# High halves of five experts' weights fetched by casting DMAs instead of cast on ScalarE

## The reference, cut to what matters

```
h = layernorm(layernorm(patches) @ W_proj + b_proj)          # 576 x 192
h = h + attention(norm(h))                                     # 12 heads, cos() queries, 9 tokens an image
h = h + experts(norm(h)):                                      # 8 experts, top 2 of each token
      logits = x @ router.T;  top_w = softmax(top 2 logits)
      for e in range(8):
          out += (silu(x @ Wg[e].T) * (x @ Wu[e].T)) @ Wd[e].T * w_e
```

## Time and profile before

| | |
|---|---|
| median of 3 runs | 222.52 us (221.71 to 222.67) |
| the profiled execution's own time | 222.33 us |
| its span | 220.4 us, mean granted clock 0.961 |
| PE busy | 190.8 us (87%) |
| DVE busy | 150.8 us (68%) |
| ACT busy | 134.2 us (61%) |
| POOL busy | 131.4 us (60%) |
| DMA | 36.34 MB, mean 165 GB/s |

### The profile page before, as it was taken

The page is one execution under the profiler, slowest core; times in us unless marked ns, Lnnn a source line. Parts: engine busy times, 40 slices in busy tenths (PEclk is TensorE's granted clock), DMA queues, the critical chain, the costliest instruction groups (busy, mean ns, idle before and its releaser), DMA issues. The chain is left out here.

```text
span 220.4 us, 4927 instructions
## 1 busy us (share of the span) xinstructions
PE 190.8 (87%) x1575; PEld 144.4 (66%) x1589; DVE 150.8 (68%) x486; ACT 134.2 (61%) x315; POOL 131.4 (60%) x184
## 2 busy tenths in 40 slices
PE   8999969999697798699578989996999999999940
PEld 2899959999596664464154667673777666667620
DVE  1799798997983899887558977775755555555420
ACT  2654587599969698666868667564544444444430
POOL 8342399999699434869988976784222222222222
PEclk9999999999999999985969999999999999999985
DMA  5999999949852512573787777753511112222111
GB/s 154 372 398 382 355 408 408 386 162 308 240 146 49 150 52 66 149 212 100 203 281 213 239 175 189 191 123 58 118 19 18 20 19 45 42 42 45 18 21 18
DMA packets 22577, 36.34 MB, mean 165 GB/s; under 512 B 4057, under 2 KB 11545, under 8 KB 22553
## 3 DMA queue, kind: packets, MB, share of 16 engines
q1 hardware_dynamic: 19609, 33.26, 47.2%
q0 software_dynamic: 2944, 2.76, 8.6%
HBM read 31.65 MB, written 4.36 MB: 163 GB/s over the span
## 5 line engine op out<-in xcount | busy, mean ns | idle before, releaser
L1383 PE MATMUL ps<-experts 128*117 128x193 f32 (+1 forms) x320 | 54.4, 328 | 0.5 <-ACT experts L816 0.3
L1383 PEld LDWEIGHTS ps<-experts 128*117 128x117 f32 (+1 forms) x320 | 52.1, 180 | 2.0 <-DMA experts<-x_t 1.5
L430 POOL TENSOR_TENSOR experts<-stage,experts 128x528 bf16<-128x528 f32 x36 | 43.2, 1216 | 13.5 <-ACT experts L741 12.8
L1318 DVE TENSOR_TENSOR shared<-shared,ps 128x256 f32<-128x256 f32 x48 | 20.2, 421 | 36.9 <-ACT shared L925 35.3
L741 ACT CAST experts<-stage 128x528 f16<-128x528 f32 x64 | 38.8, 633 | 5.2 <-DMA stage<-w_exp 5.2
L925 ACT ACTIVATE shared<-ps 128x256 f32<-128x256 f32 x48 | 18.5, 385 | 28.4 <-PE ps L1588 26.9
L725 ACT ACTIVATE experts<-experts 128x468 f32<-128x468 f32 x39 | 21.9, 586 | 15.4 <-POOL experts L561 4.0
L685 POOL DMA_INDIRECT out<-shared x8 | 12.4, 1545 | 30.3 <-ACT shared L950 22.8
L561 POOL TENSOR_TENSOR experts<-experts 128x468 f32<-128x468 f32 x14 | 16.5, 1176 | 15.6 <-ACT experts L725 15.4
L685 POOL DMA_INDIRECT out<-shared,slot_row x8 | 14.2, 1775 | 19.4 <-ACT shared L950 16.3
L1609 PE MATMUL ps<-experts,shared 128*128 128x192 f16 (+1 forms) x96 | 23.7, 246 | 1.6 <-DVE shared L1323 1.6
(11 more groups left out here) (241 smaller groups left out, 369.7 us busy)
## 6 DMA issues: line engine op xcount, KB each, us to landing
stage<-w_exp SPq DMA_DIRECT2D x64, 264.0 KB
experts<-x_t SPq DMA_DIRECT2D x12, 472.0 KB, 8.0
experts<-x_t SPq DMA_DIRECT2D x16, 236.0 KB, 6.8
experts<-w_proj SPq DMA_DIRECT2D x8, 384.0 KB, 6.7
slot_x<-experts SPq DMA_DIRECT2D x1, 1032.0 KB, 8.0
shared<-slot_x SPq DMA_DIRECT2D x8, 129.0 KB, 3.3
out<-h SPq DMA_DIRECT2D x1, 351.0 KB
slot_x<-xs,posi POOLq DMA_INDIRECT x10
```

The source lines that it names most:

```text
L430: ops.tensor_tensor(lo_w[:, to + EW:to + EW + PW], stage[:, n % STAGES, :], hi_w[:, to:to + PW], ALU.subtract).then_inc(split_pool if on_p ...
L1318: v.tensor_tensor(hid[:, n % 2, :], act[:, n % 2, :], pcol(n % 3, BLK, BLK), ALU.mult).then_inc(hid_ready, 1)
L1383: last = mm(dst, xbuf[:, t % 2, k, 0:m], gw[:, k, :], start=k == 0, stop=k == KT - 1)
```

## The change

Only ScalarE's high halves of experts 0 to 2 (24 pieces) stay. For experts 3 to 7 GpSimd issues one DMA each, from the float32 weights in HBM to the float16 half in `experts`, which converts on the way. The float32 pieces of these experts are still loaded to `stage`, since the low halves need them. Their split waits for `high_in` of the expert and for its own `stage_in` in place of `hi_done`. GpSimd splits 40 pieces in place of 36. The wait for `csum_ready`, and those that guard the region of experts 4 to 7, move to GpSimd, ahead of the DMAs that write there. VectorE doubles its pieces in steps 0 to 2 only (before: 0 to 5).

```
-    POOL_PIECES = 36
+    POOL_PIECES = 40
+    ACT_EXPERTS = 3
...
+        high_in = [sem(f"high_in{j}") for j in range(ACT_EXPERTS, E)]
...
-            eng.wait_ge(hi_done, n + 1)
+            if e < ACT_EXPERTS:
+                eng.wait_ge(hi_done, n + 1)
+            else:
+                eng.wait_ge(high_in[e - ACT_EXPERTS], 16)
+                eng.wait_ge(stage_in[n % STAGES], 16 * (n // STAGES + 1))
...
+            def high_by_dma(e):
+                pool.dma_start(hi_w[:, 2 * e * EW:2 * e * EW + EW], w_exp[e, :, :]).then_inc(high_in[e - ACT_EXPERTS], 16)
...
             square_adds(4, 3, 4)
+            pool.wait_ge(csum_ready, 1)
+            for e in range(ACT_EXPERTS, EARLY):
+                high_by_dma(e)
             rests(14, 15)
             square_adds(4, 4, 6)
             rests(15, 16)
             square_adds(4, 6, NG)
-            rests(16, 24)
+            rests(16, 17)
+            wait_tok(pool, TILES - 1)
+            pool.wait_ge(ssq_done, TILES)
+            pool.wait_ge(blank_out, 48)
+            pool.wait_ge(vec_consts, 1)
+            for e in range(EARLY, E):
+                high_by_dma(e)
+            rests(17, 24)
...
-                for n in range(n0, n1):
+                for n in range(n0, min(n1, ACT_EXPERTS * NP)):
...
-                    if n == NP * EARLY:
-                        wait_tok(sc, TILES - 1)
-                        sc.wait_ge(ssq_done, TILES)
-                        sc.wait_ge(blank_out, 48)
-                        sc.wait_ge(vec_consts, 1)
...
```

In ScalarE's order the calls `high_parts(18, 19)`, `(19, 20)`, `(20, 21)`, `(21, 22)` and `(22, 23)` become `(18, 21)`, `(21, 22)`, `(22, 23)` and `(23, 24)`, the last one ahead of `turned(4)`; every later call is gone, with the loop that cast one or two pieces a step. In VectorE's loop:

```
-                for _ in range(2 if n < 6 else 1):
+                for _ in range(2 if n < 3 else 1):
```

More of the change, by code:

```diff
@@ L886, in _ @@
             repeat(1, 1)
-            high_parts(18, 19)
+            high_parts(18, 21)
             turned(2)
@@ L890, in _ @@
             turned(3)
-            high_parts(19, 20)
+            high_parts(21, 22)
             attend(3)
             table(4, ACT.Sin)
-            high_parts(20, 21)
+            high_parts(22, 23)
             cosine_of(2)
@@ L898, in _ @@
             repeat(2, 1)
-            high_parts(21, 22)
+            high_parts(23, 24)
             turned(4)
-            high_parts(22, 23)
             attend(4)
-            high_parts(23, 25)
             parts_of(0)
-            high_parts(25, 26)
             parts_of(1)
-            high_parts(26, 27)
             rows(0)
-            high_parts(27, 28)
             rows(1)
-            high_parts(28, 29)
             rows(2)
             parts_of(2)
-            high_parts(29, 32)
             both_choices(0)
-            high_parts(32, 34)
             sc.wait_ge(gap_ready, 1)
@@ L952, in _ @@
             rows_high(0)
-            high_parts(34, 39)
             both_choices(1)
-            high_parts(39, 41)
-            high = 41
             for n in range(NSTEP):
@@ L965, in _ @@
                     finish(c - 1)
-                for _ in range(2 if n < 6 else 1):
-                    if high < NP * E:
-                        high_parts(high, high + 1)
-                        high += 1
                 if n == 2:
```

## The result

| | before | after |
|---|---|---|
| median | 222.12 us (219.49 to 222.67, 4 runs) | 229.12 us (228.41 to 232.36, 4 runs) |
| ratio | | 1.0336, 95% interval 1.0268 to 1.0404 |
| profiled execution | 222.33 us, span 220.4 | 228.41 us, span 226.5 |
| mean granted clock | 0.961 | 0.941 |
| ACT busy | 134.2 us | 114.0 us |

What follows compares the result with a forecast made beforehand. TensorE bounds the kernel behind 158 us; some 6 us lie open from 105.6 to 131.4. Step 9 comes 3.3 us earlier, less 0.7 for slower loads: 222.33 - 2.6 = 219.7 us, range 217.2 to 225.0.

Steps and rivals of the forecast that it cites:

- I take 0.7 off: Expert stage, by step 9: 0.7 us off a 3.3 us gain for loads slowed beside the casting DMAs, leaving 2.6.
- The routing's shift: Before the last square sums: expert 3's DMA issue on GpSimd makes the routing 1.3 us later.
- The moved waits: GpSimd, before the issues for experts 4 to 7: waits moved there are over by then and cost nothing.
- What comes back before the stage: Before the expert stage: low_parts(2) ready earlier returns 0.4 us of TensorE's wait, so the stage begins at 106.6.
- ScalarE's relief: Start of the expert stage: without 40 casts silu(0) can start at 108.0, but gate(0), behind VectorE's pieces, at 109.9.
- Step 5 to step 9: Expert stage: these four steps take 8.2 us undisturbed in place of 9.42, putting step 9 3.3 us earlier.
- The Trainium skill's rule: VectorE pieces 40 to 43: each waits up to one GpSimd split, so gate(0) could lose what ScalarE gave.
- Slow transfers: Rival, chance 0.12: at 100 GB/s expert 5 lands at 117.3, VectorE's wait delays gate(0) to 118.9, ending at 226.1 us.
- The dear issues: Rival, chance 0.16: GpSimd's DMA issues cost 2.65 us each, routing 2.7 later, ending at 223.1 us.
- Nothing moves: Rival, chance 0.12: loads of 5 us or more hold VectorE's pieces 40 to 47, gate(3) stays: 222.0 us.
- remote waits: Rival, chance 0.18: ScalarE's waits for something the trace calls remote go with the casts; capped gain 4.5, 217.8 us.
- P: Theory made after the result, not in the prediction: GpSimd's splits and VectorE's operations hold one another up, independent of DMA.

Runs made afterwards that it cites:

- e3: Changed kernel with no casting transfers; low halves of experts 3 to 7 taken against expert 0's high half, matmuls on experts 0 to 2 only: 217.96 us, ratio 0.9886.
- e5: e3 with GpSimd's pieces 25 to 29 moved behind low_parts(0) and low_parts(1): 216.29 us, ratio 0.984.
- e4: Changed kernel with issues apart: expert 4's unmoved, 5's ahead of piece 24, 6's behind low_parts(2), 7's behind GpSimd's last piece; whole-row packets: 229.19 us, ratio 1.0327.
- e8: Kernel before, no casting transfers, with only GpSimd's pieces 25 to 29 moved behind low_parts(0) and low_parts(1): 219.39 us, ratio 0.9941.
- e11: e8 with gate(0) also put ahead of VectorE's first two pieces: 223.24 us, ratio 1.0077.
- e1: Changed kernel with each casting transfer made two, over even and odd eighths of the row, so runs are 528 values long: 222.90 us, ratio 1.011.
- e7: e6 with expert 3's transfer issued behind the last square sum: 220.95 us, ratio 1.0033.
- e9: e6 with transfers for experts 4 to 7 only, ScalarE casting 32 pieces, nothing issued ahead of the square sums: 220.91 us, ratio 0.9948.
- e10: e9 with gate(0) put ahead of VectorE's first two pieces: 219.54 us, ratio 0.9878.
- e12: e7 with gate(0) put ahead of VectorE's first two pieces: 221.68 us, ratio 0.999.
- e6: e1 with GpSimd's pieces 25 to 29 moved behind low_parts(0) and low_parts(1): 221.74 us, ratio 1.0085.
- e2: Changed kernel with plain float32 transfers, no conversion, written over both halves of the expert; matmuls on experts 0 to 2 only: 226.02 us, ratio 1.0256.

## Why the prediction was wrong

**The step that failed** is "I take 0.7 off, because the casting DMAs still run beside the loads until 120 and a load of 3.6 us becomes some 4.3". I had added rates (190 GB/s beside the 134 that flow, under a bound of 320) and so found room for both. The runs show that the two queues share the engines by turns of packets, not by rates: the loads fell to 0.80 MB in 22 us, 36 GB/s, and to a median of 17.3 us. The transfers took more than I gave them (4.10 MB written in 22 us, so 8.2 MB read, 373 GB/s), and all of it at the loads' cost. The time, 228.41 us, lies above even the range's end of 225.0. The earlier trace rows held the warning: q1 moves 33.26 MB in 19609 packets, 1.7 KB each, and a row of the new transfer is 16.9 KB. I looked at the price of an issue for such a row, never at what its packet does to the others.

**From there on the sum is wrong in sign.** The routing's shift was nearly right: first_norm(2) at 72.29, 1.14 later (1.3 forecast). The moved waits, put at nothing, cost 1.15 us, and the cheap issues made up for it. "What comes back before the stage" (0.4) was TensorE idle for 5.96 us instead, and the start 111.53, not 106.6. ScalarE's relief was right as a cause: its next silu waits for TensorE alone. But gate(0) at 117.85 (109.9 forecast) waited for VectorE's pieces; I had named that order of waits and mis-sized the load in it. Step 5 to step 9 took 8.14 us, where I had 8.2. So by step 9 the forecast is 7.4 us off (136.15 against 128.8): 4.9 at the start and 3.2 between steps 0 and 5, less the 0.7 that I had taken off, which didn't fall in 5 to 9. Another 1.5 came in steps 9 to 21.

**The Trainium skill's rule** ("SBUF — State Buffer", "Who interferes with whom") I had weighed at VectorE's pieces. The measured cost lay elsewhere, and larger: 4.45 us for four normalizing operations in place of 1.25 (e3 and e5), 7.15 for one of five elements (e4). The rule says the later instruction blocks until the other is done; in e4 it was held through nearly all seven splits. In the kernel after the starved loads hid this, as GpSimd had gaps.

**The rivals.** Slow transfers (226.1) comes nearest in time, and by the wrong victim: the last expert had landed by about 101 us (120 forecast), and no split waited for its high half. Their packets were late for nobody and made the pieces late. The dear issues fell: 0.55 to 0.76 us. Nothing moves fell too. On the remote waits: one stayed in the kernel after (3.21 us at 157.19 on ScalarE), where no cast was left in that stage, and they are absent from the profiles of e8 and e11 with all their casts; so the casts don't make them. They are absent from e1 to e7 too, and there in e9, e10 and e12 (1.65 to 3.05 us). What makes them is open; the groups were on different chips.

**What e3 and e5 say of the idea.** The change without its transfers is worth 2.6 us (e3), 4.0 with the order mended (e5), of which the order alone gave 0.9 in the kernel before (e8). The transfers with the best packets I tried cost about that: e5 to e6, 216.29 to 221.74, is 5.5 us, of it some 0.8 for the place of expert 3's issue. Only with one transfer fewer does anything stay (e9, and more with the gate first, e10), and how much of that is the order's isn't settled.

**Open:** whether the transfers gain anything over e8; what e10 still loses around steps 2 to 5; a packet size between 528 and 4224 values wasn't tried; and whether e4's loss is all P.

## What to carry to other kernels

Before a bulk transfer is set beside latency-bound loads, compare their packets, not their rates: with both queues busy each got as many packets as the other here, so a row of 4224 values beside rows of 528 took eight ninths of the engines. Cut the bulk transfer's rows to the loads' size, and send no more of it than pays. When an engine is fed better, look at what its unbroken run blocks beside it. And when an experiment mends the order as well, run the kernel before with that order alone, or the gain goes to the wrong change.

## What the runs showed of the hardware

- Two queues with work took turns by packet: 1465 to 1467 packets in 15 us (e7), 680 to 680 in 7 us (e1), and 366 to 363 in 15 us with rows of 4224 and of 528 values (after).
- A row of 4224 values was on an engine for 0.59 us, a run of 528 values for 0.849 x 22 x 16 / 3037 = 0.098 us. Eight of these make 0.79, but packets of one queue overlap (1188 of them gave a share of 121.7% in 77 to 83 us of e1, alone), so the price in bytes is smaller: with both queues busy, whole rows and loads read 6.3 MB in 15 us (after), 420 GB/s, short runs and loads 2.67 MB in 7 us (e1), 381 GB/s.
- The conversion cost nothing to be seen: 0.59 us a row with it (16.9 KB read, 8.4 written), 0.57 without (e2).
- An issue by GpSimd of a 2.16 MB transfer took 0.55 to 0.76 us, of half of that in four runs a row 0.74 (5.90 us for eight in e1).
- Beside back-to-back GpSimd splits a VectorE operation could wait for more than one of them: 7.15 us for 117x5 elements beside seven (e4).
- TensorE, after 3.48 us of idle time, ran at the lower clock from 73 to 78 us (e6), and 24 matmuls took 1.40 us in place of 0.81 (e7, after 1.40 us idle, clock 1.00).
